# Layer norm, routing and places of half 0 first, those of half 1 beneath half 0's scatters; additions of the mean on VectorE

## The reference

```python
x = x + conv(_ln_c(x))                       # FFT, gain, inverse FFT, 64 -> 16 -> 64 channels
t = _to_tokens(x)                            # 8 x 1024 tokens of 64
n = (t - mean(t)) / sqrt(var(t) + 1e-5)
logits = einsum('bsd,de->bse', n, gate_w) + gate_b
top_probs, top_idx = top_k(softmax(logits), 2);  top_probs /= sum(top_probs)
hidden = silu(einsum(n, w1[e])) * einsum(n, w2[e])
out = sum over the two experts of top_probs * einsum(hidden, w3[e])
x = _from_tokens(t + out)
```

## Time and profile before

| what | value |
|---|---|
| median of 3 runs | 589.88 us (589.6 to 590.0) |
| profiled execution | 589.5 us, of which the span from the first to the last instruction is 587.7 us |
| GpSimd busy | 287.6 us (49%) |
| TensorE busy | 214.6 us (37%), weight loads 174.4 us |
| VectorE busy | 163.5 us (28%) |
| ScalarE busy | 105.8 us (18%) |
| 128 scatters, line 980 | 125.0 us busy, 977 ns each |
| mean granted TensorE clock | 0.623 of full speed |

### The profile page before, as it was taken

The page is one execution under the profiler, slowest core; times in us unless marked ns, Lnnn a source line. Parts: engine busy times, 40 slices in busy tenths (PEclk is TensorE's granted clock), DMA queues, the critical chain, the costliest instruction groups (busy, mean ns, idle before and its releaser), DMA issues.

```text
span 587.7 us, 5198 instructions
## 1 busy us (share of the span) xinstructions
PE 214.6 (37%) x1607; PEld 174.4 (30%) x1608; DVE 163.5 (28%) x281; ACT 105.8 (18%) x172; POOL 287.6 (49%) x293
## 2 busy tenths in 40 slices
PE   5586693020000311001799841010178795000000
PEld 5364682000000310000787740000077684000000
DVE  4945678982000000000233300000024435011011
ACT  5746562100000100000332210000033231000000
POOL 1480237477777777774000067777400001777772
PEclk9777655555555555555699965555567996555555
DMA  8990000000000600000011161111000112111111
GB/s 297 248 397 9 1 1 0 11 23 27 25 27 25 204 29 25 27 27 18 19 52 41 69 205 26 27 27 27 17 19 37 37 55 92 43 45 27 43 45 30
DMA packets 20940, 35.26 MB, mean 60 GB/s; under 512 B 5788, under 2 KB 6172, under 8 KB 20276
## 3 DMA queue, kind: packets, MB, share of 16 engines
q1 hardware_dynamic: 12468, 26.51, 13.3%
q0 software_dynamic: 8288, 8.41, 6.0%
q10 hardware_dynamic: 160, 0.01, 0.0%
HBM read 18.13 MB, written 16.78 MB: 59 GB/s over the span
## 4 chain that ended last, share of the span: by engine, by line
issue 42%; PE 26%; DVE 16%; POOL 11%; ACT 3%; DMA 1%; another core or an unknown queue 1%; POOLq 0%; ACTq 0%; DVEq 0%
POOL scratch L985 10%; PE banks L671 7%; PE banks L661 5%; PE banks L662 5%; PE banks L645 2%; PE banks L528 1%; DVE ct L726 1%; PE banks L561 1%; PE banks L548 1%; PE banks L503 1%; DVE pwc L766 1%; DVE ssq L729 1%; DVE m L832 1%; DVE top L832 1%
## 5 line engine op out<-in xcount | busy, mean ns | idle before, releaser
L980 POOL DMA_INDIRECT sorted_x<-shared,place x128 | 125.0, 977 | 49.7 <-issue 38.7
L905 DVE SCALAR_TENSOR_TENSOR power<-banks,fold 128x512 f32<-128x512 f32 x40 | 27.5, 691 | 304.0 <-remote 178.6
L985 POOL DMA_INDIRECT scratch<-sorted_y,place x64 | 61.3, 958 | 97.6 <-DMA sorted_y<-enh 78.4
L985 POOL DMA_INDIRECT xs<-sorted_y,place x64 | 60.5, 946 | 85.0 <-DMA sorted_y<-filt 65.8
L661 PE MATMUL banks<-shared,w_hi 128*128 128x128 f16 x320 | 63.5, 243 | 51.0 <-issue 50.9
L662 PE MATMUL banks<-shared,w_lo 128*128 128x128 f16 x320 | 63.9, 241 | 48.6 <-issue 47.4
L671 PE MATMUL banks<-w_all,power 128*128 x320 | 50.6, 301 | 41.4 <-issue 40.6
L671 PEld LDWEIGHTS banks<-w_all,power 128*128 128x128 f32 x320 | 46.9, 219 | 45.2 <-issue 45.2
L456 ACT COPY shared<-banks 128x1024 f16<-128x1024 f16 x20 | 20.2, 1012 | 206.3 <-PE banks L645 106.6
L661 PEld LDWEIGHTS banks<-shared,w_hi 128*128 x320 | 35.6, 111 | 58.2 <-issue 54.2
L662 PEld LDWEIGHTS banks<-shared,w_lo 128*128 x320 | 34.6, 108 | 56.1 <-issue 54.0
(11 more groups left out here) (144 smaller groups left out, 337.1 us busy)
## 6 DMA issues: line engine op xcount, KB each, us to landing
sorted_x<-zeros SPq DMA_DIRECT2D x2, 2560.0 KB, 29.7
w_raw<-sorted_x SPq DMA_DIRECT2D x20, 256.0 KB, 2.9
w_raw<-in_L_ffn_w SPq DMA_DIRECT2D x5, 512.0 KB, 16.1
sorted_y<-filt SPq DMA_DIRECT2D x10, 256.0 KB, 2.0
sorted_y<-enh SPq DMA_DIRECT2D x10, 256.0 KB, 2.0
xs<-in_x SPq DMA_DIRECT2D x8, 256.0 KB, 5.1
sorted_x<-shared,place POOLq DMA_INDIRECT x128
out<-cen_sq SPq DMA_DIRECT2D x8, 256.0 KB
```

The costliest lines, as they stand in the source:

```text
L905: nc.vector.scalar_tensor_tensor(hid[:, q % RING, :], bank[2 + q % 2], HSCALE / WSCALE, gated[:, q % 2, :], ALU.mult, ALU.mult).then_inc(h ...
L980: nc.gpsimd.indirect_dma_start(out=sorted_x[k], out_offset=bass.IndirectOffsetOnAxis(ap=place[:, k, j, t:t + 1], axis=0), in_=parts[:, HT ...
L985: nc.gpsimd.indirect_dma_start(out=yg[k][:, j, t, :], out_offset=None, in_=sorted_y[k], in_offset=bass.IndirectOffsetOnAxis(ap=place[:, k, ...
```

## The change

The three loops of layer norm (VectorE, ScalarE and TensorE) are cut into two, one for each half, which on VectorE is followed by the half's routing and places. So VectorE's order is now: layer norm of blocks 0 to 3, `route(0)`, `places_of(0)`; layer norm of blocks 4 to 7 with the low parts of these blocks (`low`), the tokens' means, `route(1)`, `places_of(1)`; owners and weights of both; and last the eight additions of the mean (`add_mean`). TensorE runs `ranks(0)` behind `logits(3)` and `ranks(1)` behind `logits(7)`. As half 1's blocks now pass banks 0 to 5 after `ranks(0)`, these ranks use banks 6 and 7 (`RANK_AT`), and the logits of half 1, which write bank 7, wait for `place_done` of half 0. GpSimd writes the low parts of blocks 0 to 3 alone and then goes to the scatters; those of half 0 wait for four low parts, those of half 1 for all.

```diff
+RANK_AT = (6, 2)
@@ ScalarE
-            for n in range(NBLK + 3):
-                if n < NBLK:
+            def normalize(first, last, n):
+                if n < last:
...
+            for h in range(HALVES):
+                for n in range(HB * h, HB * (h + 1) + 3):
+                    normalize(HB * h, HB * (h + 1), n)
@@ TensorE
             def logits(n):
                 pe.wait_ge(xp_done, n + 1)
+                if n == HB:
+                    pe.wait_ge(place_done, 1)
...
                 transpose_parts(n)
-                if n >= 1:
+                if n % HB:
                     logits(n - 1)
...
-            logits(NBLK - 1)
-            pe.wait_ge(id16_set, 2)
-            for k in range(HALVES):
-                ranks(k)
+                if n % HB == HB - 1:
+                    logits(n)
+                    ranks(n // HB)
@@ VectorE
+            def low(n):
+                dve.wait_ge(hi_done, n + 1)
+                nc.vector.tensor_tensor(parts[:, BT * n:BT * (n + 1), 1, :], tok[:, n % 2, :, :], parts[:, BT * n:BT * (n + 1), 0, :],
+                                        ALU.subtract).then_inc(lo_done, 1)
...
+            def add_mean(n):
+                dve.wait_ge(mean1_done, 1)
+                nc.vector.tensor_tensor(ct_cen[:, 4 * n:4 * n + 4, :, :], ct_cen[:, 4 * n:4 * n + 4, :, :],
+                                        per_tile(mean1[:, BT * n:BT * (n + 1)], C), ALU.add).then_inc(x1t_done, 1)
...
-            for k in range(HALVES):
-                route(k)
-                places_of(k)
+            for n in range(HB + 2):
+                normalize(0, HB, n)
+            route(0)
+            places_of(0)
+            for n in range(HB, NBLK + 3):
+                normalize(HB, NBLK, n)
+                if n >= HB + 3:
+                    low(n - 3)
+            token_means()
+            route(1)
+            places_of(1)
             for k in range(HALVES):
                 owners_of(k)
                 weights(k)
+            for n in range(NBLK):
+                dve.wait_ge(tok_done, n + 1)
+                add_mean(n)
@@ GpSimd
-            for n in range(NBLK):
+            for n in range(HB):
                 pool.wait_ge(hi_done, n + 1)
...
-            pool.wait_ge(mean1_done, 1)
-            for n in range(NBLK):
-                pool.wait_ge(tok_done, n + 1)
-                nc.gpsimd.tensor_tensor(ct_cen[:, 4 * n:4 * n + 4, :, :], ct_cen[:, 4 * n:4 * n + 4, :, :],
-                                        per_tile(mean1[:, BT * n:BT * (n + 1)], C), ALU.add).then_inc(x1t_done, 1)
...
-            pool.wait_ge(lo_done, NBLK)
             for k in range(HALVES):
+                pool.wait_ge(lo_done, HB * (k + 1))
                 pool.wait_ge(place_done, k + 1)
```

More of the change, by code:

```diff
@@ L32 @@
 PTILES = TILES // 2
+HB = NBLK // 2
 TOKW = P + 2 * M + 2
@@ L432, in _ @@
                                          ACT.Square).then_inc(censq_done, 1)
-                if 1 <= n <= NBLK:
+                if first < n <= last:
                     cols = slice(BT * (n - 1), BT * n)
@@ L583, in logits, with ranks @@
                 last.then_inc(lg_done, 1)
+            def ranks(k):
+                pe.wait_ge(id16_set, 2)
+                pe.wait_ge(chosen_done, k + 1)
+                totals, counts = bank[4 + k][0:ENTRIES, 0:E], bank[4 + k][:, E:2 * E]
+                for e in range(E):
+                    last = nc.tensor.matmul(totals[:, e:e + 1], chosen[:, k, e, :, :].rearrange("p j t -> p (j t)"), ones[:, 0:1],
+                                            start=True, stop=True)
+                last.then_inc(totals_ps, 1)
+                halves = [chosen[:, k, g * E // 2:(g + 1) * E // 2, :, :].rearrange("p e j t -> p (e j t)") for g in range(2)]
+                for g in range(2):
+                    nc.tensor.matmul(bank[RANK_AT[k] + g], below[:, :], halves[g], start=True, stop=False)
+                pe.wait_ge(totals_out, k + 1)
+                nc.tensor.matmul(counts, ones[0:ENTRIES, :], total_runs[:, k, :], start=True, stop=True).then_inc(counts_ps, 1)
+                pe.wait_ge(runs_done, k + 1)
+                for g in range(2):
+                    last = nc.tensor.matmul(bank[RANK_AT[k] + g], ones[0:ENTRIES, :],
+                                            runs[:, k, g * E // 2:(g + 1) * E // 2, :].rearrange("p e r -> p (e r)"), start=False, stop=True)
+                last.then_inc(places_ps, 1)
             keep_warm(2, bank[3])
@@ L797, in _, with normalize @@
                 nc.vector.tensor_tensor(pairs[:, a, 1, :], fold1[:, a, 0, :], fold1[:, a, 1, :], ALU.subtract).then_inc(enh_done, 1)
-            for n in range(NBLK + 2):
-                if n < NBLK:
+            def normalize(first, last, n):
+                if n < last:
                     dve.wait_ge(cen_ps, n + 1)
@@ L809, in _ @@
                                             AX_X, ALU.add).then_inc(ssq_done, 1)
-                if n >= 2:
+                if first + 2 <= n < last + 2:
                     b = n - 2
@@ L872, in places_of @@
                 dve.wait_ge(places_ps, k + 1)
-                step(nc.vector.tensor_tensor(places, bank_pairs[k][:, :, :].rearrange("p g (e r) -> p (g e) r", r=ENTRIES),
+                step(nc.vector.tensor_tensor(places, bank_pairs[RANK_AT[k] // 2][:, :, :].rearrange("p g (e r) -> p (g e) r", r=ENTRIES),
                                              first[:, k, :].unsqueeze(2).to_broadcast([P, E, ENTRIES]), ALU.add))
```

30 lines of the change are left out of this document (7 added, 23 removed).

## The result

The changed kernel takes 604.96 us (median of 4 runs, 603.3 to 605.7), the kernel before 589.83 beside it: ratio 1.0253, with a 95% interval of 1.0231 to 1.0274. The profiled execution took 605.7 us with a span of 603.9. The forecast was 609.0, within 600 to 618, and slower.

What follows compares the result with a forecast made beforehand. It took GpSimd's indirect DMA issue, with TensorE at about 2.8 us per matmul beneath it, as the bound. Half 1's first scatter moves from 193.2 to 212.8: 589.5 + (212.8 - 193.2) = 609.1 us, range 600 to 618.

Steps and rivals of the forecast that it cites:

- Half 0 first: Layer norm, routing and places of blocks 0 to 3 first: place_done(0) at 97.7, 11.5 us earlier, first scatter 98.6.
- 64 scatters, 82.8 us: GpSimd's scatters of half 0 last 82.8 us as before, from 98.6 to 181.4.
- TensorE beneath them: TensorE's 141 matmuls for half 1 lie beneath half 0's scatters and aren't through when these end at 181.4.
- the first 20 or so are free there too: Under half 0's scatters TensorE's first 20 or so matmuls run at full speed before it slows.
- about 56 of 141: How far TensorE is through half 1's matmuls when half 0's scatters end at 181.4; block 6 not through.
- half the pace: Rival, slower all the same: matmuls beneath scatters cost 1.4 us, number 80 to 85 at 181, 608 us; within the forecast's 0.84.
- Release: TensorE flows again 8.7 us after half 0's last scatter, at 190.1; two ScalarE copies and logits(7) add 2.9 us.
- Routing 1, places 1: VectorE's half 1 work after logits(7): 8.96 us, then 9.95 with ranks; half 1's first scatter at 212.8, before 193.23.
- The rest shifted whole: After half 1's first scatter, two half stages, gathers and stores keep their length and move by 212.8 - 193.2.
- slow pace: TensorE beneath GpSimd's scatters or gathers takes about 2.8 us per matmul, until shortly after the last one; cause unknown.
- full pace: Rival, faster: TensorE isn't slowed beneath half 0's scatters, GpSimd has no gap, everything moves by -11.5 to 578.0; chance 0.12.

Runs made afterwards that it cites:

- chip 14: Changed kernel unedited, run again beside the kernel before on another chip of the 590 us kind: 603.4 us against 589.69, ratio 1.0235.
- chips 0, 5 and 6: Chips where the kernel before takes 449 to 450 us; the changed kernel, unedited on the first of them, took 438.59 us, ratio 0.9743.
- chip 10: Changed kernel with GpSimd waiting for both halves' places before its first scatter, on a chip of the 590 us kind: 613.86 us against 589.74, ratio 1.0391.
- three kernels: Kernel before (589.83 us), changed kernel (604.96 us), and changed kernel with no scatter before both halves' places (613.86 us).
- a fourth: Changed kernel with layer norm of blocks 4 and 5 ahead of routing 0, 69 matmuls left beneath the scatters: 586.86 us against 589.69 before, ratio 0.9952.

## Why the prediction held, step by step

The time and the mechanism held: TensorE's work of half 1 was held up beneath the scatters and let go behind them. How many matmuls come through was mis-sized, and the sign depended on something that the prediction didn't know of.

*Half 0 first*: held. Place_done of half 0 came at 98.68 for 97.7. In this execution the first transposes already stand 1.2 us later than in the kernel before (67.69 for 66.47), which no edit precedes; without that, layer norm would have been 0.2 us ahead of the forecast. Routing 0 took 8.97 for 8.96, places 0 as before; first scatter 99.56 for 98.6, inside the stated 98 to 100. The reason given for 8.96, the additions alone, was short: of the 4.57 us, 3.7 are theirs.

*64 scatters, 82.8 us*: measured 81.25. The 82.8 included the two slowed scatters of the earlier trace rows, and VectorE's work that slowed them stands beside half 1's scatters now, as the prediction itself said.

*TensorE beneath them*: right in kind, mis-sized in number. That "the first 20 or so are free there too" rested on the 21 matmuls of ranks(1), and the "about 56 of 141" was taken from the expert stage. In the changed kernel the signal of block 6, number 64, came at 131.00, and the trace holds 104 matmuls by 154.14; block 7's signal, number 88, was the first awaited one to miss the scatters. On chip 14 number 88 came in time (173.44) and that of the logits behind it, number 120, missed them. The statement that "ScalarE's copy of block 6 comes only after the scatters" was wrong; it was block 7's. What happened is nearer to the rival "half the pace", which had number 80 to 85 at the end of the scatters, block 6 through and block 7 not, and 608 us. The conclusion stood because any missing signal waits for the same moment; the prediction had said that the outcome hardly depends on the pace.

*Release*: 8.7 us behind the last scatter predicted, 9.08 measured (180.81 to 189.89). As block 6 was through, one copy and logits(7) were left, 1.70 us instead of 2.9.

*Routing 1, places 1*: 8.97 and 9.52 for 8.96 and 9.95; first scatter of half 1 at 210.84 for 212.8; gap 30.03 us for 31.4 (212.8 - 181.4).

*The rest shifted whole*: 605.7 - 210.84 = 394.9 us behind that scatter, before 589.5 - 193.23 = 396.3. So 1.4 us of the 3.4 between 609.1 and 605.7 lie here, and 2.0 ahead of it. The additions were not hidden with 5 us to spare, as the prediction said, but stood directly ahead of the first product; what hid the delay was TensorE's slow pace behind it.

*The rivals*: "full pace", at 0.12, is what the second kind of chip does: -11.5 us was its price, -11.0 was measured. The prediction gave as its condition something that the expert and gather stages alone have. What decides is the kind of chip. No row of one trace from one chip could say that, and the chance stood for the wrong uncertainty: that the forecast of "slower" came true is in part luck, as the comparison was made on the kind that the trace of before came from. The Trainium skill's sentence that "PE and ACT never wait on anyone" (SBUF — State Buffer, Who interferes with whom) is said of the engines' ports to SBUF. The traces from chips 0, 5 and 6 show nothing against it. On chip 10 TensorE's work is held up by the scatters (block 7's copy at 113.30 without them, at 189.89 beside them on the chip of the comparison), by what no run shows, so the sentence couldn't exclude the hold-up, and the runs don't refute it.

## What to carry to other kernels

Before work is put beneath GpSimd's indirect DMAs, look in the trace for signals of TensorE that arrive long after the matmuls they stand for; where there are such, what waits for one of them may wait until some 9 us behind the end of the DMAs, and a chain that leads from there back to GpSimd opens a gap. Time such a change on several chips: here the same edit is 2.4 to 2.5% slower on one kind and 2.6% faster on the other. What didn't lose on either was to do half of the dependent part ahead of the first DMA, in the idle time of the engines: 0.5% faster on one kind, 2.7% on the other.

## What the runs showed of the hardware

- Two kinds of chip, for one program: 449 to 450 us on three chips, 590 on two (and on the one of the comparison). Scatters are issued at the same pace on both, one every 1.26 us; the difference that the traces show is TensorE's pace beneath them, 180 matmuls in 20 us against 8. The cause is open, and so is whether it belongs to the chip or to its condition.
- On the first kind a signal of TensorE can be 67 us late (transposes issued by 122.8, copy at 189.89), while signals that don't come from TensorE are quick in the same stretch: ScalarE's cast ends at 114.13 and VectorE, which waits for it, starts at 114.17; ScalarE's copy ends at 132.01 and TensorE starts at 132.07.
- The hold-up outlasts the last scatter: by 8.4 to 9.1 us in three kernels, by 15.1 in a fourth, and for 6 us of that in the kernel before GpSimd is idle and no DMA engine moves anything.
- One two-input VectorE instruction of 0.42 us took 1.26 beside a GpSimd tensor_tensor of 1.15 us, which writes a low part.
